# A graph layer's aggregation stage: who posts the updates of TensorE's mixer products

## The chip, the core and the metric

The kernel runs on one core of a Trainium2 chip. TensorE (PE in the profile) multiplies, with PEld for its weight loads; VectorE is DVE, ScalarE is ACT, GpSimd is POOL, SyncE is SP. Each engine has a sequencer of its own, which reads the instructions in order and hands matmuls, copies and so on to the engine; waits, register work and branches it does by itself. The metric is the device time of one execution in microseconds, lower is better.

## The reference

One layer of a graph network on 6250 nodes with 256 features, float32. Cut to what matters here:

```python
xn = layernorm(x)
# message passing: 100000 edges, sorted by dst
agg = segment_sum(xn[src], dst)
gnn = relu(xn @ W_self + (agg / max(deg, 1)) @ W_neigh + b)
# linear attention over all nodes, with a gate
k = softmax(k, axis=nodes); context = k^T v (per head); out = q @ context
gate = sigmoid(gelu(xn' @ Wg1 + bg1) @ Wg2 + bg2)
mix = out * gate @ Wproj + bproj
x = x + gnn + mix
# then a mixture of experts, routed by a graph attention over 131072 other edges
x = x + ffn(layernorm(x))
```

## The kernel before

The program is a row of stages; in one of them, `aggregate`, three strands run side by side, about from 105 to 1375 us of the execution.

**Message passing.** POOL gathers rows of the table `xn_tab` by indirect DMA (L857): one gather brings 128 rows (one "sub-step") into a ring of 4 x 8 slots, `msg`. ACT builds for each half of 8 sub-steps the one-hot matrices `hot` that say to which node of a tile each row belongs (`prep`, L1301 and L1303). TensorE multiplies the two (`steps`, L1125): two sub-steps are accumulated in one of four PSUM banks, and the last matmul of the pair counts up `s_mm`. DVE adds the bank to its tile of `acc` (`sums`, L879) and counts up `s_acc`, which frees the bank. One call `steps(.., u, u+4)` is four sub-steps, two banks. It has its addresses from a table: TensorE's sequencer loads them into registers (L1114, L1120), checks them, waits for the bank (L1123), and sets up each pair (L1125). POOL may overwrite a quarter of the ring once `s_mm` says that its rows were used (its wait is in the middle of each half, and in the same place it tells TensorE by `s_landed` that the half before has landed).

**The mixer** (the attention with its gate, and `x @ W_self`). Its products are put between the calls of `steps`, in program order, on two PSUM banks `mix[0]` and `mix[1]`:

- Stage B of this text, 220 to 565 us, 7 groups of 7 tiles: `kv(g, u)` (L1142 and L1145) makes k and v of 128 nodes in `mix[0]`. ACT reads them (`taken`, L1312 to L1314: the exponential, a copy, v scaled) and counts up `s_ev`; then `context` (L1152) multiplies the pair, and the next `kv` may write `mix[0]`. The order is `steps`, `kv(u)`, `context(u-1)`, `steps`, ..., with 8 calls of `steps` in a group.
- Stage C, 565 to 1190 us, 7 groups of 2 halves (4 and 3 tiles): `hidden` (L1162; DVE scales it, ACT makes the gelu), `gates` twice (L1170; ACT makes the sigmoid), `attention` twice (L1179; DVE multiplies it with the gate, `gated`, L887), then `output` for each tile (L1194 and L1196; DVE adds it up, `rowed`, L903). A call of `steps` stands ahead of each of them but for the second `attention`, 8 calls in a half.

After 1190 us the rest of the message passing runs alone (`rest`). The last matmul of each product carries the update of the semaphore that its reader waits for (`.then_inc`).

**A sort** of the other graph's edges on DVE, between its `sums`, with transposes on TensorE (`turn_from`, L304).

DVE and ACT do their work in one written order too: a `sums` that waits for `s_mm` holds up the `rowed` behind it.

Of the kernel before, what the change touches and what calls it, by code (L numbers as in the profile page):

```python
# [15 lines left out]
P = 128  # L16
# [669 lines left out]
def aggregate(c, a, t, acc, plan, xnT, r2, base):  # L686
# [8 lines left out]
    nc = c.nc  # L695
# [4 lines left out]
    with ctx:  # L700
# [16 lines left out]
        wg2 = sb("wg2", [GATE_H, D])  # L717
# [24 lines left out]
        for _, n in HALF:  # L742
# [10 lines left out]
        mix = [ps(f"mx_ps{i}", [P, 512]) for i in range(2)]  # L753
        s_w, s_wq, s_wqc, s_kv, s_ev, s_ctx, s_bd, s_m, s_msb = (c.sem("mx_" + n) for n in (
            "w", "wq", "wqc", "kv", "ev", "ctx", "bd", "m", "msb"))
# [5 lines left out]
        s_hgp, s_hg, s_gp, s_gate, s_at, s_prod, s_rows, s_copied = (c.sem("mx_" + n) for n in (  # L761
            "hgp", "hg", "gp", "gate", "at", "prod", "rows", "copied"))
# [20 lines left out]
        with nc.Block() as block:  # L783
# [324 lines left out]
            def _(pe):  # L1108
# [28 lines left out]
                def kv(g, u):  # L1137
                    at = (g * GT + u) * P
                    pe.wait_ge(s_ev, g * GT + u + 1)
                    b = mix[0]  # L1140
                    for k in range(KC):
                        nc.tensor.matmul(b[:, :], xnT[:, k, at:at + P], wqkv[:, k, D:3 * D], start=(k == 0), stop=False,  # L1142
                                         skip_group_check=True)

                    nc.tensor.matmul(b[:, 0:D], c.ones[0:1, :], ncm[:], start=False, stop=True,  # L1145
                                     skip_group_check=True).then_inc(s_kv, 1)

                def context(g, u):

# [6 lines left out]
                def hidden(g, i):  # L1156
                    n = HALF[i][1] * P
                    pe.wait_ge(s_in[i], 48 * g + 48)

                    pe.wait_ge(s_copied, g * GT + HALF[i][0] + GT)  # L1160
                    for k in range(KC):
                        last = nc.tensor.matmul(mix[0][0:GATE_H, 0:n], wg1[:, k, :], xT[i][:, k, :], start=(k == 0),  # L1162
                                                stop=(k == KC - 1))
                    last.then_inc(s_hgp, 1)

                def gates(g, i, h):
                    n = HALF[i][1] * P

                    pe.wait_ge(s_hg, 2 * g + i + 1)
                    nc.tensor.matmul(mix[1 - h][:, 0:n], wg2[:, h * P:(h + 1) * P], hg[:, 0:n], start=True,  # L1170
                                     stop=True).then_inc(s_gp, 1)

                def attention(g, i):
                    n = HALF[i][1] * P
                    for h in range(KC):

                        pe.wait_ge(s_gate, 4 * g + 2 * i + h + 1)
                        for k in range(KC):
                            last = nc.tensor.matmul(mix[1 - h][:, 0:n], m_sb[:, k, h * P:(h + 1) * P], xT[i][:, k, :],  # L1179
                                                    start=(k == 0), stop=(k == KC - 1))  # L1180
                        last.then_inc(s_at, 1)

                def output(g, i, j):
                    u = HALF[i][0] + j
                    at = j * P
                    b = mix[j % 2]
                    if j == 0:

                        pe.wait_ge(s_prod, 2 * g + i + 2)
                    elif j >= 2:  # L1190

                        pe.wait_ge(s_copied, g * GT + u - 1 + GT)
                    for k in range(KC):
                        nc.tensor.matmul(b[:, D:2 * D], xT[i][:, k, at:at + P], wself[:, k, :], start=(k == 0), stop=(k == KC - 1))  # L1194
                    for k in range(KC):
                        last = nc.tensor.matmul(b[:, 0:D], prod[:, k, at:at + P], wproj[:, k, :], start=(k == 0), stop=(k == KC - 1))  # L1196
                    last.then_inc(s_rows, 1)

                pe.sem_inc(s_mm, 2 * JB)
                pe.sem_inc(s_kv, GT)  # L1200
# [5 lines left out]
                                 skip_group_check=True)  # L1206
                pe.wait_ge(s_w, 16 * W_LOADS)
                for k in range(KC):
                    for h in range(KC):
                        last = nc.tensor.transpose(mix[0][:, h * D + k * P:h * D + (k + 1) * P], wqkv[:, k, h * P:(h + 1) * P], c.ident[:])  # L1210
                last.then_inc(s_wq, 1)
                nc.tensor.transpose(psS[0:TILES, 0:P], r2[:], c.ident[:])
                for k in range(KC):
                    last = nc.tensor.matmul(psS[0:GATE_H, 512:513], wg1[:, k, :], ln_b[:, k:k + 1], start=(k == 0), stop=(k == KC - 1))
# [13 lines left out]
                for p in range(LANE_PAIRS):  # L1228
                    for k in range(QUART):
                        for i in range(2):  # L1230
# [4 lines left out]
                            elif at == CHUNKS:  # L1235
                                pe.wait_ge(s_kmax, KC * CHUNKS + 1)
                                for h in range(KC):
                                    last = nc.tensor.transpose(psS[0:1, h * P:(h + 1) * P], cmax[:, h:h + 1], c.ident[:])
                                last.then_inc(s_k, 1)
                pe.wait_ge(s_kmax, KC * CHUNKS + 2)  # L1240
                for g in range(GROUPS):
                    for u in range(GT + 1):
                        steps(LANE_PAIRS + g, u // 2, u % 2 * 4, u % 2 * 4 + 4)
                        if u < GT:
                            kv(g, u)
                        if u:
                            context(g, u - 1)

                pe.wait_ge(s_bd, 1)
                for k in range(KC):  # L1250
                    for h in range(KC):
                        last = nc.tensor.matmul(mix[0][:, k * D + h * P:k * D + (h + 1) * P], wqT[:, h, k * P:(k + 1) * P], ctxbd[:, h, :],
                                                start=True, stop=True)
# [4 lines left out]
                for g in range(GROUPS):  # L1258
                    for i in range(2):
                        p = C_PAIR + 2 * g + i  # L1260
                        steps(p, 0, 0, 4)
                        if i == 0:
                            srt.turn_from(pe, 0, 2 * g + 1)
                        hidden(g, i)
                        steps(p, 0, 4, 8)
                        gates(g, i, 0)
                        steps(p, 1, 0, 4)
                        gates(g, i, 1)
                        steps(p, 1, 4, 8)
                        attention(g, i)  # L1270
                        for j in range(4):
                            steps(p, 2 + j // 2, j % 2 * 4, j % 2 * 4 + 4)
                            if j < HALF[i][1]:
                                output(g, i, j)
                            if i == 0 and j == 2:
                                srt.turn_from(pe, 1, 2 * g + 2)
# [1232 lines left out]
```

## Time and profile before

| | |
|---|---|
| three runs | 2709.36, 2723.76, 2723.77 us, median 2723.76 |
| the profiled execution | 2707.9 us, its span 2706.1 us |
| busy, of the span | PE 72%, PEld 50%, DVE 44%, ACT 34%, POOL 55% |
| mean granted TensorE clock | 0.827 |
| matmuls | 7528 records; a float32 product is recorded as two |

The page of the profile gives one execution. The busy share of an engine is the part of the span in which one of its instructions was in work. For an instruction that waited, the profile names what ended the idle time of its engine ("releaser"); "issue" means that no wait ended just then, the sequencer was only now ready with it; "remote" means that the semaphore was counted up at that time, but that no instruction that counts it up had ended near then. The ends of matmuls are modelled.

### The profile page before, as it was taken

The numbers are of one execution on the slowest core, as the hardware profiler recorded it, in microseconds if no ns is written. First come the engines' busy times: TensorE is split into PE (matmuls) and PEld (weight loads), VectorE is DVE, ScalarE is ACT, GpSimd is POOL, SyncE is SP. The second block draws the span as 40 slices with busy tenths as digits, with TensorE's granted clock in tenths as the row PEclk, the third lists the DMA queues.
The fourth block names the chain that finished last, engine by engine and source line by source line (L and its number), as shares of the span: only waits on it lengthen the run. The fifth ranks groups of instructions, "written<-read, shape, count | busy, mean of one in ns | idle before, by whom it ended". The sixth has DMA issues, their size and how long they took to land. (4 is left out here: it accounts for less than half of the span.)

```text
span 2706.1 us, 26735 instructions
## 1 busy us (share of the span) xinstructions
PE 1941.8 (72%) x7528; PEld 1341.2 (50%) x7528; DVE 1194.9 (44%) x2204; ACT 907.0 (34%) x1994; POOL 1480.2 (55%) x1512
## 2 busy tenths in 40 slices
PE   5687878876677777765455888788888788784235
PEld 4454545454455554543345555456555555553223
DVE  6353222345455555543386223324235143346368
ACT  3432444444444444443323222222323222222124
POOL 2455655666566666676602566666666666561510
PEclk9888988998888898887665899999998889897555
DMA  5443222244343434353358221212222112215544
GB/s 182 142 134 114 87 70 79 84 118 137 113 137 111 139 120 143 105 166 123 93 161 277 82 49 36 70 36 49 57 50 56 38 48 56 51 36 172 160 149 152
DMA packets 197046, 282.83 MB, mean 105 GB/s; under 512 B 43024, under 2 KB 147443, under 8 KB 195762
## 3 DMA queue, kind: packets, MB, share of 16 engines
q0 software_dynamic: 61280, 115.13, 16.6%
q1 hardware_dynamic: 97218, 121.11, 13.5%
q10 hardware_dynamic: 38416, 44.96, 5.1%
q8 instruction: 67, 1.10, 0.2%
q14 instruction: 65, 0.53, 0.1%
HBM read 195.29 MB, written 85.80 MB: 104 GB/s over the span
## 5 line engine op out<-in xcount | busy, mean ns | idle before, releaser
L857 POOL DMA_INDIRECT ag_msg<-xn_tab,step_src x784 | 784.8, 1001 | 462.1 <-issue 218.3
L1814 POOL DMA_INDIRECT edge_rows<-hx_d,gat_src x648 | 623.7, 962 | 357.1 <-issue 180.6
L1125 PE MATMUL ag_ps<-ag_msg,ag_hot 128*128 x1760 | 491.5, 428 | 117.4 <-issue 61.0
L2002 PE MATMUL ex_psY<-co_rows 128*128 128x256 f32 x1568 | 416.0, 426 | 130.9 <-ACT co_rows L2056 70.2
L1125 PEld LDWEIGHTS ag_ps<-ag_msg,ag_hot 128*128 128x128 f32 x1760 | 364.4, 215 | 244.2 <-issue 187.6
L879 DVE TENSOR_TENSOR acc<-acc,ag_ps 128x257 f32 x440 | 186.0, 423 | 638.3 <-remote 276.5
L2002 PEld LDWEIGHTS ex_psY<-co_rows 128*128 128x128 f32 x1568 | 332.2, 215 | 212.3 <-ACT co_rows L2056 79.9
L1990 PE MATMUL ex_psF<-co_rows 128*128 128x448 f32 x896 | 353.9, 551 | 46.2 <-DMA ex_b<-in_b_dram 24.9
L1301 ACT ACTIVATE gat_self<-iota_row,step_nloc 128x128 f32<-128x128 f32 x880 | 270.4, 388 | 304.4 <-issue 164.7
L1928 DVE TENSOR_TENSOR hi_one_low<-hi_numbers,hi_low 128x2048 bf16<-128x2048 f32 x64 | 146.4, 2287 | 498.9 <-remote 416.1
L1990 PEld LDWEIGHTS ex_psF<-co_rows 128*128 128x128 f32 x896 | 171.2, 194 | 212.5 <-issue 165.3
L2056 ACT COPY co_rows<-ex_psY 128x256 f32<-128x256 f32 x196 | 71.3, 373 | 471.7 <-PE ex_psY L2002 245.7
L2049 ACT ACTIVATE co_rows<-ex_psF,ex_b 128x448 f32<-128x448 f32 x224 | 137.8, 633 | 252.8 <-PE ex_psF L1990 167.8
L1142 PE MATMUL mx_ps<-wqkv,xnT 128*128 128x512 f32 x196 | 103.3, 653 | 47.2 <-ACT gat_dst L1314 37.6
L1303 ACT ACTIVATE ag_hot<-gat_self,ones 128x1024 f32<-128x1024 f32 x110 | 126.3, 1149 | 13.0 <-issue 5.3
L1929 DVE TENSOR_TENSOR hi_one_high<-hi_numbers,hi_high 128x1568 bf16<-128x1568 f32 x64 | 114.0, 1781 | 0.0
L1194 PE MATMUL mx_ps<-wself,xnT 128*128 128x256 f32 x196 | 57.8, 421 | 39.2 <-DVE xnT L903 27.6
L218 DVE TENSOR_TENSOR gatsort_keys<-gatsort_keys 128x512 f32<-128x512 f32 x117 | 80.3, 687 | 1.0
L1142 PEld LDWEIGHTS mx_ps<-wqkv,xnT 128*128 128x128 f32 x196 | 40.1, 210 | 80.9 <-ACT gat_dst L1314 40.8
L219 DVE TENSOR_TENSOR gatsort_keys<-gatsort_keys 128x512 f32<-128x512 f32 x117 | 80.1, 684 | 0.0
L1312 ACT ACTIVATE gat_dst<-mx_ps 128x256 f32<-128x256 f32 x49 | 18.8, 383 | 179.0 <-remote 88.4
L1224 PE MATMUL srt_ps<-xnT,wqkv 128*128 128x448 f32 x112 | 49.7, 588 | 20.9 <-DVE bmax L916 15.0
(377 smaller groups left out, 2000.0 us busy)
## 6 DMA issues: line engine op xcount, KB each, us to landing
y_d<-co_rows ACTq DMA_DIRECT2D x28, 896.0 KB
co_rows<-y_d SPq DMA_DIRECT2D x28, 896.0 KB, 9.5
ag_msg<-xn_tab,step_src POOLq DMA_INDIRECT x784
xnT<-base_d SPq DMA_DIRECT2D x7, 1792.0 KB
edge_rows<-hx_d,gat_src POOLq DMA_INDIRECT x648
base_d<-xnT ACTq DMA_DIRECT2D x7, 1024.0 KB
sums_d<-edge_rows SPq DMA_DIRECT2D x5, 1344.0 KB
xg<-in_x_dram SPq DMA_DIRECT2D x7, 896.0 KB, 5.7
```

The lines of the kernel that those rows point to most:

```text
L857: pool.indirect_dma_start(msg[:, q, u, 0:D], None, c.xn_tab, bass.IndirectOffsetOnAxis(ap=t.idx[:, at:at + 1], axis=0)).then_inc(s_g[q], 16)
L879: V.tensor_tensor(own, own, bank[(at // JOIN + u) % BANKS][:, 0:ROWW], ALU.add).then_inc(s_acc, 1)
L1125: last = nc.tensor.matmul(bank[(at + r) % BANKS][:, 0:ROWW], hot[:, k, u0 + r * JOIN + j, :], ring[:, j * ROWW:SLOTS * ROWW][:, ds(places[ ...
L1142: nc.tensor.matmul(b[:, :], xnT[:, k, at:at + P], wqkv[:, k, D:3 * D], start=(k == 0), stop=False, skip_group_check=True)
L1301: A.activation(dif[:, u, :], c.iota_row[:], ACT.Abs, bias=t.nloc[:, ds(half * SHALF + u, 1)])
L1303: A.activation(hot[:, k], dif[:], ACT.Relu, bias=c.ones[:, 0:1], scale=-1.0).then_inc(s_hot, 1)
L1814: pool.indirect_dma_start(G[:, j % RING, w, :], None, c.hx_d, bass.IndirectOffsetOnAxis(ap=plan.idx[:, at + w:at + w + 1], axis=0)).then_i ...
L1928: V.tensor_tensor(one_low[:, k % 2], bcast(numbers, 1, HIST), bcast(low[:, at], 2, P), ALU.is_equal)
L1929: V.tensor_tensor(one_high[:, k % 2], bcast(numbers[:, 0:HIGHS], 1, HIST), bcast(high[:, at], 2, HIGHS), ALU.is_equal).then_inc(s_one, 1)
L1990: last = nc.tensor.matmul(psF[i % FB][:, 0:HB], w1[:, e, k, (i // 2) * P:(i // 2 + 1) * P], yT[:, k, (i % 2) * HB:(i % 2 + 1) * HB], start ...
L2002: last = nc.tensor.matmul(bank[:, 0:D], hh[:, k].rearrange("p a b -> p (a b)")[:, u * P:(u + 1) * P], w2[:, e, k, :], start=(k == 0), stop ...
L2049: nc.scalar.activation(hh[:, i // 2, i % 2, :], psF[i % FB][:, 0:HB], ACT.Gelu, bias=b1[:, e * HC + i // 2:e * HC + i // 2 + 1]).then_inc( ...
```

## The change

In five products the last matmul no longer carries the update. Instead TensorE's sequencer waits until the engine has drained, and then counts the semaphore up itself.

```diff
@@ kv
                     nc.tensor.matmul(b[:, 0:D], c.ones[0:1, :], ncm[:], start=False, stop=True,
-                                     skip_group_check=True).then_inc(s_kv, 1)
+                                     skip_group_check=True)
+                    pe.drain()
+                    pe.sem_inc(s_kv, 1)
@@ hidden
-                    last.then_inc(s_hgp, 1)
+                    pe.drain()
+                    pe.sem_inc(s_hgp, 1)
@@ gates
-                    nc.tensor.matmul(mix[1 - h][:, 0:n], wg2[:, h * P:(h + 1) * P], hg[:, 0:n], start=True,
-                                     stop=True).then_inc(s_gp, 1)
+                    nc.tensor.matmul(mix[1 - h][:, 0:n], wg2[:, h * P:(h + 1) * P], hg[:, 0:n], start=True, stop=True)
+                    pe.drain()
+                    pe.sem_inc(s_gp, 1)
@@ attention
-                        last.then_inc(s_at, 1)
+                        pe.drain()
+                        pe.sem_inc(s_at, 1)
@@ output
-                    last.then_inc(s_rows, 1)
+                    pe.drain()
+                    pe.sem_inc(s_rows, 1)
```

The updates of `steps` (`s_mm`), of `context` (`s_ctx`) and of the sort's transposes stay on their matmuls. No instruction changes its place.

## Rows read from the trace of the kernel before

**Rows 1.** The gathers by their line: ns min/median/max, first and last start in us.
```profile
L857 POOL DMA_INDIRECT ag_msg<-xn_tab,step_src x784: 940/946/2321, 105.6 to 1351.0; - x196
```

**Rows 2.** Windows: length, busy us of PE, PEld, DVE, ACT, POOL, granted clock, DMA, GB/s.
```profile
220.00:565.00 345.00, 277.75 (x962) 170.25 (x960) 104.94 (x213) 153.41 (x410) 207.25 (x209) 0.89 0.31 90
565.00:1190.00 625.00, 464.02 (x1625) 319.40 (x1624) 327.26 (x582) 267.72 (x570) 399.20 (x394) 0.85 0.41 123
```

**Rows 3.** Timeline of TensorE, one unit of stage B: start, us, instruction, idle before.
```profile
403.71 1.88 PE L1142 MATMUL mx_ps<-wqkv,xnT 128*128 128x512 f32 x4
405.52 0.69 PE L1145 MATMUL mx_ps<-ncm,ones 1*128 1x256 f32 x2
406.14 0.71 PE L1152 MATMUL mx_ps<-gat_dst 128*128 128x129 f32 x4
406.69 1.90 PE L1125 MATMUL ag_ps<-ag_msg,ag_hot 128*128 x8
408.43 1.88 PE L1142 MATMUL mx_ps<-wqkv,xnT 128*128 128x512 f32 x4
```

**Rows 4.** Timeline of TensorE, a stall of stage B.
```profile
379.82 0.69 PE L1145 MATMUL mx_ps<-ncm,ones 1*128 1x256 f32 x2
...
380.99 1.90 PE L1125 MATMUL ag_ps<-ag_msg,ag_hot 128*128 x8
394.42 1.22 PE L1142 MATMUL mx_ps<-wqkv,xnT 128*128 128x512 f32 x1 [11.52 <-ACT gat_dst L1314]
```

**Rows 5.** Timeline of ACT in the same stretch.
```profile
393.52 0.38 ACT L1312 ACTIVATE gat_dst<-mx_ps 128x256 f32<-128x256 f32 x1 [12.92 <-remote]
```

**Rows 6.** Timeline of POOL in the same stretch.
```profile
389.85 0.95 POOL L857 DMA_INDIRECT ag_msg<-xn_tab,step_src  x1 [0.30 <-issue]
404.68 1.17 POOL L857 DMA_INDIRECT ag_msg<-xn_tab,step_src  x1 [13.89 <-PE ag_ps L1125]
```

**Rows 7.** Who waited for whom in stage B: us in total, times, longest.
```profile
ACT gat_dst L1312 <- remote: 88.4, 13, 17.6
DVE acc L879 <- remote: 86.1, 17, 12.6
POOL ag_msg L857 <- PE ag_ps L1125: 63.2, 13, 13.9
```

**Rows 8.** Who waited for whom in stage C.
```profile
POOL ag_msg L857 <- PE ag_ps L1125: 78.6, 25, 10.8
PE mx_ps L1170 <- ACT xnT L1320: 29.1, 5, 8.6
PE mx_ps L1194 <- DVE xnT L903: 27.6, 8, 11.6
PE mx_ps L1162 <- DVE xnT L903: 15.7, 4, 8.7
```

**Rows 9.** TensorE's sequencer at the lines of steps: ns min/median/max of each instruction.
```profile
L1114 PEldq TENSOR_LOAD <-step_table x203: 502/713/3027, 120.7 to 1366.0; - x102
L1120 PEldq TENSOR_LOAD <-step_table x203: 472/477/1504, 121.3 to 1366.6; - x102
L1120 PEldq FUSED_REGOPS  x203: 151/151/162, 121.9 to 1367.1; - x102
L1123 PEldq EVENT_SEMAPHORE  x203: 51/51/51, 122.2 to 1367.4; - x102
L1125 PEldq FUSED_REGOPS  x228: 42/44/46, 222.3 to 553.0; - x114
```

**Rows 10.** Timeline of TensorE in stage C, a product that had to be waited for.
```profile
758.95 1.12 PE L1170 MATMUL mx_ps<-xnT,wg 64*128 64x512 f32 x2 [1.07 <-issue]
760.75 1.56 PE L1125 MATMUL ag_ps<-ag_msg,ag_hot 128*128 x6 [0.68 <-issue]
```

**Rows 11.** TensorE's drain at the aggregation's end, by its line.
```profile
L783 PEldq DRAIN  x1: 1268/1268/1268, 1372.4 to 1372.4; - x1
```

**Rows 12.** Timeline of TensorE, its last matmuls before that drain's end.
```profile
1371.60 2.00 PE L1125 MATMUL ag_ps<-ag_msg,ag_hot 128*128 x8 [1.94 <-DVE acc L879]
```

## The prediction

> **What bounds the kernel now.** I read the page first, then windows over the aggregation, the timelines of single units, and the waits. Only the aggregation is touched, and no other stage runs beside it, so the change is worth what it makes stages B and C longer or shorter; a shift of their end moves everything after it alike.
>
> POOL issues 784 gathers of 0.95 us [rows 1] with 0.30 between them [rows 6], so 1.25 us each or 980 us in all, from 105.6 to 1351.0 us [rows 1], a stretch of 1245 us. It is not the bound alone: in stages B and C it waited 63.2 and 78.6 us for matmuls of `steps` [rows 7, 8]. TensorE is busy 278 of 345 us in stage B and 464 of 625 us in stage C [rows 2]; its idle time there is 67 + 161 = 228 us. A unit of stage B without a stall takes 408.43 - 403.71 = 4.72 us, back to back [rows 3], against 5.0 us of POOL for the four gathers that it uses. 49 such units would be 231 us, so a good part of stage B's 345 us is stalls.
>
> The stalls look odd. In one, the last matmul of `kv` ends at 380.51 us [rows 4], but ACT, which has nothing else to wait for, starts its read at 393.52, 13.0 us later, and the profile calls the releaser "remote" [rows 5]: the semaphore counted up then, with no matmul near. TensorE in turn sits 11.5 us for ACT [rows 4]. POOL made gathers back to back up to 390.8 [rows 6]. The updates that ride on matmuls thus arrive late at times, while TensorE itself goes on (the eight matmuls of `steps` started at 380.99). Waits that end so cost ACT 88.4 us and DVE 86.1 us in stage B [rows 7]. This is what the change can win.
>
> The Trainium skill (PSUM — Partial Sum Buffer, "Engine vs sequencer instructions") says that updates attached to an engine's instruction fire when it completes, and wants them there; the trace disagrees in this stage by 13.0 us. By that rule the change would win nothing and pay all of the price below.
>
> **The change, part by part.** It removes 49 + 14 + 28 + 28 + 49 = 168 updates from matmuls (kv, hidden, gates, attention, output) and adds as many drains and sequencer updates.
>
> *The update itself.* A sequencer's semaphore instruction takes 0.05 us (the 51 ns of L1123) [rows 9]. A drain shown ends at 1372.4 + 1.27 = 1373.67, and the matmuls before it at 1373.60 [rows 11, 12]: it adds under 0.1 us after the last matmul. An update of the mixer then reaches ACT or DVE some 0.1 us after the product, if the drain does not wait for late updates too and the sequencer's own are on time. Neither is to be seen before; the rivals take that up.
>
> *The lost run-ahead.* This is the price. The sequencer's work for one call of `steps` is, up to its first matmul, 713 + 477 + 151 + 51 + 44 = 1436 ns of instructions [rows 9], and with the gaps between them 1.80 us, read where a product had to wait until 758.95 and its sequencer with it: the next `steps` began at 760.75, 0.68 us after the product's end although nothing was to be waited for [rows 10]. In a flowing unit these 1.8 us are hidden, since the sequencer does them while earlier matmuls run [rows 3]. A drain holds the sequencer at the end of the product, so that all of it is bare, about 1.9 us with drain and update. Whatever product stands between is hidden behind it: after `kv` comes `context`, whose own start after the drain and 0.7 us of matmuls [rows 3] leave some 1.6 us of added length.
>
> - kv, stage B: 49 x 1.6 = 78 us.
> - hidden 14, gates 28, the second attention 14, output 49: 105 followed by `steps`, x 1.9 = 200 us.
> - the first attention, 14, followed by matmuls without table loads: what is left of 1.9 us without the 1.44 us of sequencer work, 0.46, so 6 us.
>
> Sum 284 us more of TensorE's time. Where the product had to be waited for anyway, part of this is paid already (the 0.68 us of rows 10), and it counts as idle time now.
>
> *What takes it up.* If all idle time of the two stages were filled, they would last 278 + 78 = 356 instead of 345 us and 464 + 206 = 670 instead of 625 us: +11 and +45, together +56 us. Stalls are idle time that ends with POOL's pause, not with TensorE's work, so bare sequencer time ahead of one costs little, and the mixer's own late updates go. But not all idle time can be filled: the updates of `steps` stay on their matmuls, and DVE and ACT meet those waits in their written order, ahead of the `rowed` and `gated` that TensorE waits for (27.6 and 15.7 us on L903, 29.1 us on ACT) [rows 8]. I leave 14 us of it, which makes +70 us.
>
> *The bounds.* Above: nothing is taken up, +284 us. Below: the granted clock is 0.89 and 0.85 in the two stages [rows 2], a mix of its full and its half level; had it been full, the busy time would be about 278 x 0.89 = 247 and 464 x 0.85 = 394 us, and with the drains 325 and 600 us against 345 and 625: -45 us. Long idle stretches were followed by the slow level (the `steps` after the stall), short ones of 1.9 us need not be.
>
> DVE, ACT and POOL get no new work. POOL finds the slots freed later where TensorE is later, and pauses more; behind a pause the updates are on time (the two matmul updates of rows 3 released ACT at once), which works against the stalls and is part of why I let most idle time be filled. The rest of the aggregation after 1190 us has no mixer and only shifts.
>
> **The numbers.** The sum goes against the profiled execution: 2708 + 70 = 2778 us. The runs lie at 2709 and twice at 2724, so half their spread above it: **2785 us**. What a measurement can tell from no change is about 0.5%, 14 us.
>
> **Rivals.**
>
> 1. *Faster.* The mixer's updates come at once, the chain product, reader, next product no longer breaks, TensorE is never idle for long and keeps its full clock. The stages then run at the lower bound, -45 us: 2663 in the profile, about 2670. For it: 88.4 us of waits of ACT on late updates in stage B alone [rows 7]. Against it: even without a single stall the drained unit of stage B is 4.7 + 1.6 = 6.3 us, and a group of 8 calls about 47 us against 49 now, so that little is there to win, and the late `s_mm` remain. It decides where the clock returns to full level in both stages. Chance 0.20.
> 2. *No change.* The filled idle time and half of the clock's return meet: +56 - 50 = about 0, 2720. Chance 0.13.
> 3. *The change does not do what it says.* The drain waits until the late updates of `steps` are out as well, or TensorE's sequencer posts into the same jam. Then each late update stops the whole of TensorE at the next drain, where it now ran on for a unit (the eight matmuls of rows 4). The skill's page says a drain waits until the engine is fully idle, and leaves open whether unposted updates count. Half of the idle time at most is then filled: 284 - 114 = +170 us, 2886; with a quarter, 284 - 57 = +227, 2943. For it: in the drain shown the last update was not late, so nothing speaks against. Chance 0.19.
>
> My own case, slower by 15 to 130 us with 2785 in the middle, gets 0.48. The first rival gives faster 0.20, the second same 0.13, mine and the third slower 0.67. The range leaves out the lower half of the first rival and the far end of the third: 2685 to 2930 us.
>
> **What would show it.** In the timeline of TensorE a unit of stage B from `kv` to `kv` of 6.2 to 6.5 us instead of 4.72, with an idle time of 1.0 to 1.3 us before L1125 put down to "issue", and after each output 1.8 to 2.0 us of it; "PE ag_ps L1125 <- issue" as the longest wait of both stages, near 200 us. ACT L1312 <- remote gone. DVE acc L879 <- remote still there. Both stages within a few us of 360 and 670. Wrong would be: a drain after whose matmuls the update still comes microseconds late (then rival 3), an idle time before L1125 under 1 us after outputs (the price is too high), or a granted clock of 0.95 and more with stages under 340 and 615 us (rival 1).

## The result, and the profile after

The changed kernel takes 2915.99 us (median of 4 runs, 2904.72 to 2933.57) against 2723.77: ratio 1.0746, 95% interval 1.07 to 1.0793. Slower, as forecast, but by 192 us where 61 were forecast. The profiled execution has a span of 2915.2 us. Ratios, here and below, are those on record, taken over fast runs alone; the quotient of two medians can differ from them by up to 0.4% (here it is 1.0706).

The windows of stages B and C, with the boundaries put at the last product of each (length, busy us of PE, PEld, DVE, ACT and POOL, granted clock, DMA share, GB/s), first before the change, then after it:

```profile
220.00:572.00 352.00, 282.14 (x978) 173.70 (x976) 107.33 (x218) 153.41 (x410) 211.53 (x213) 0.89 0.31 92
572.00:1185.00 613.00, 457.45 (x1601) 314.40 (x1600) 324.45 (x577) 267.72 (x570) 391.14 (x385) 0.86 0.41 122
```
```profile
220.00:617.00 397.00, 304.66 (x980) 189.12 (x979) 108.01 (x218) 153.75 (x410) 211.13 (x213) 0.88 0.28 82
617.00:1409.00 792.00, 542.01 (x1600) 355.35 (x1598) 327.68 (x582) 267.05 (x570) 395.94 (x390) 0.80 0.32 96
```

Stage B is 45 us longer, stage C 179. Two things stand out: the idle time of TensorE, and its busy time, which should not have changed at all, since the matmuls are the same; in stage C its clock is 0.80 instead of 0.86.

A unit of stage B in TensorE's timeline (start, us, instruction, idle before it), to be held against [rows 3]:

```profile
302.58 0.69 PE L1145 MATMUL mx_ps<-ncm,ones 1*128 1x256 f32 x2
303.36 0.71 PE L1154 MATMUL mx_ps<-gat_dst 128*128 128x129 f32 x4
305.30 2.00 PE L1125 MATMUL ag_ps<-ag_msg,ag_hot 128*128 x8 [1.23 <-issue]
307.13 1.88 PE L1142 MATMUL mx_ps<-wqkv,xnT 128*128 128x512 f32 x4
308.94 0.69 PE L1145 MATMUL mx_ps<-ncm,ones 1*128 1x256 f32 x2
```

From `kv` to `kv` it is 308.94 - 302.58 = 6.36 us, where 6.2 to 6.5 were forecast. Behind an output, three units in stage C (eight matmuls of `steps` take 3.41 us in the first, most of it at the slow level of the clock, and 2.00 us in the second):

```profile
932.55 3.41 PE L1125 MATMUL ag_ps<-ag_msg,ag_hot 128*128 x8 [1.92 <-issue]
...
939.89 2.00 PE L1125 MATMUL ag_ps<-ag_msg,ag_hot 128*128 x8 [1.93 <-issue]
...
945.54 5.42 PE L1125 MATMUL ag_ps<-ag_msg,ag_hot 128*128 x16 [1.92 <-issue]
```

1.92 us, where 1.8 to 2.0 were forecast. All such idle time of TensorE from 220 to 606 us, from 606 to 1410 us (us in total, times, longest), and, for later, in both stages of e5 below, the changed kernel once more:

```profile
PE ag_ps L1125 <- issue: 77.4, 51, 10.4
```
```profile
PE ag_ps L1125 <- issue: 249.9, 107, 13.9
```
```profile
PE ag_ps L1125 <- issue: 267.1, 154, 3.9
```

That is 327 us, where the forecast had near 200 and the longest wait of both stages; DVE's wait for the matmuls of `steps` is longer in stage B. Who waited for whom there:

```profile
ACT gat_dst L1318 <- PEq L1147: 207.1, 44, 17.9
DVE acc L879 <- PE ag_ps L1125: 205.2, 83, 6.0
POOL ag_msg L857 <- PE ag_ps L1125: 120.4, 22, 9.7
...
DVE acc L879 <- remote: 23.7, 6, 11.4
```

ACT's waits on "remote" [rows 7] are gone, and L1147, the drain, is what releases it; but the longest such wait is still 17.9 us, and POOL waits twice as long as before. Why, the drain of `hidden` tells, first by its line and then with TensorE and DVE around it:

```profile
L1166 PEldq DRAIN  x14: 1468/3835/14842, 613.1 to 1363.3; - x14
```
```profile
1057.84 1.93 PE L1164 MATMUL mx_ps<-xnT,wg 128*64 128x512 f32 x4
1073.63 1.65 PE L1125 MATMUL ag_ps<-ag_msg,ag_hot 128*128 x3 [13.86 <-issue]
```
```profile
1071.85 0.68 DVE L910 TENSOR_TENSOR xnT<-mx_ps,xnT 64x512 f32<-64x512 f32 x1 [12.69 <-PEq L1166]
```

The product ends at 1059.77, the update of the sequencer behind it releases DVE at 1071.85, 12.1 us later. The drain, too, can be late. By the trace 21 of the 168 drains end over 0.1 us after the last matmul ahead of them and 12 over 1 us; all lateness together is 65 us.

### The profile page after: what moved, and what is told of

The parts are those of the page before. It is cut to its first block and busy times, and to the rows that moved or that the text cites. A ratio compares the mean times of both kernels' runs of the same rounds, so it can differ in the third digit from the quotient of the medians.

```text
span 2915.2 us, 26903 instructions
## 1 busy us (share of the span) xinstructions
PE 2038.8 (70%) x7528; PEld 1390.0 (48%) x7528; DVE 1197.2 (41%) x2204; ACT 905.3 (31%) x1994; POOL 1479.6 (51%) x1512
## 3 DMA queue, kind: packets, MB, share of 16 engines
q1 hardware_dynamic: 97218, 121.11, 12.6%
## 5 line engine op out<-in xcount | busy, mean ns | idle before, releaser
L857 POOL DMA_INDIRECT ag_msg<-xn_tab,step_src x784 | 784.1, 1000 | 676.2 <-PE ag_ps L1125 425.5
L1125 PE MATMUL ag_ps<-ag_msg,ag_hot 128*128 x1760 | 581.4, 489 | 409.5 <-issue 363.9
L1125 PEld LDWEIGHTS ag_ps<-ag_msg,ag_hot 128*128 128x128 f32 x1760 | 403.8, 239 | 577.6 <-issue 508.2
L879 DVE TENSOR_TENSOR acc<-acc,ag_ps 128x257 f32 x440 | 186.2, 423 | 817.5 <-PE ag_ps L1125 543.9
L1876 DVE TENSOR_TENSOR edge_rows<-edge_rows,gs_ex 128x1792 f32<-128x1792 f32 (+2 forms) x7 | 11.9, 1702 | 118.8 <-ACT gs_ex L2071 118.8
```

The costliest lines, as they stand in the source:

```text
L857: pool.indirect_dma_start(msg[:, q, u, 0:D], None, c.xn_tab, bass.IndirectOffsetOnAxis(ap=t.idx[:, at:at + 1], axis=0)).then_inc(s_g[q], 16)
L879: V.tensor_tensor(own, own, bank[(at // JOIN + u) % BANKS][:, 0:ROWW], ALU.add).then_inc(s_acc, 1)
L1125: last = nc.tensor.matmul(bank[(at + r) % BANKS][:, 0:ROWW], hot[:, k, u0 + r * JOIN + j, :], ring[:, j * ROWW:SLOTS * ROWW][:, ds(places[ ...
```

## The experiments

All ratios are to runs of the kernel before beside them. One thing surprised at once: in the first two sets the kernel before takes 2263 and 2266 us, in the last two 2687 and 2717, though the median instruction takes as long (a gather 0.946 us, the addition on L879 0.423 us, a matmul record of `steps` 0.380 us in either). The four sets ran on four chips, each on one, so that chip, host and hour cannot be told apart; the chip of the first pair is not on record. I call them places without and with late updates, because that is what tells them apart, as e5 and e9 show.

### First set: before at 2263 us

**e1_drain_only**, in all five products alike:

```diff
-                    last.then_inc(s_rows, 1)
+                    last.then_inc(s_rows, 1)
+                    pe.drain()
```

> The five products keep their update on the last matmul, and TensorE's sequencer only drains behind it; nothing else is changed. Theory (the drain's lost run-ahead is the price, the sequencer's own update a return): the price is paid whole and the late updates are back, so slower than the changed kernel, 2940 to 3000 us, with about 1.9 us of idle time before the steps behind each output. Rival (the sequencer's update is itself the slow part): like the kernel before, or at most 2800 us.

Measured: 2574.46 us, ratio 1.1381 (1.1352 to 1.1409). The absolute range was set for the other place; as a ratio it was 1.08 to 1.10, and the result lies above that too. Nor is it slower than the change: e5 below gives the change there 1.1377: with the update on the matmul or by the sequencer, the same. Where no update is late the drain alone is the price, and the sequencer's update is worth nothing.

**e2_kv_only**: `drain` and `sem_inc` behind `kv`, the other four as before.

> Only kv drains and posts by the sequencer; the 119 products of stage C keep their update on the matmul. The profile of the changed kernel has stage B 41 us longer and stage C 180 us longer. Theory (the two stages pay for themselves): 2750 to 2765 us, 25 to 45 us above before. Rival (the drains in stage B let POOL and TensorE enter stage C in another phase, and part of the 180 us comes from there): 2790 us or more.

Measured: 2355.72 us, ratio 1.043 (1.0405 to 1.0455). Outside both absolute ranges; e5 and e6 show that the stages do pay for themselves. Each pays more in this place: stage B is 377 us here against the 278 us of e6, 99 more, where the first pair had 45.

**e3_ahead_drained** splits `steps` into the register loads and the rest, and asks for the next call's registers before the product:

```diff
-                def steps(p, k, u0, u1):
+                def ready(p, k, u0, u1):
...
+                    count = pe.value_load(t.half[:, ds(at + n - 1, 1)], min_val=1, max_val=HALVES)
+                    return half, at, n, k, u0, places, count
...
-                        steps(p, 0, 4, 8)
+                        call = step(call)
                         gates(g, i, 0)
```

`step(call)` runs a call and returns the registers of the next.

> As the changed kernel, but the register loads and checks of the next call of steps are issued before the product and its drain instead of behind them. Theory (the bare 1.4 us of table loads per drain is the price): the idle time before steps behind an output falls from 1.92 to about 0.5 us, stages B and C lose some 49 x 1.2 + 105 x 1.4 = 206 us, less where POOL becomes the bound: 2690 to 2740 us. Rival (the drain itself or a jam of updates is the price): 2850 us or more.

**e4_ahead_only**: the same without the drains.

> The kernel before with the same early register loads and no drain. Theory: the loads are hidden in flowing units already, so within 15 us of before, a little faster where a product had to be waited for (0.68 us of idle time each): 2695 to 2725 us. Rival (late updates dominate what happens after each wait): no difference at all.

Measured: e3 2265.66 us, ratio 1.0012 (1.0001 to 1.0023); e4 2259.19 us, 0.9987 (0.9974 to 1.0). As ratios, both are as the theory had it. The 168 drains are still there in e3; without the bare register loads behind them the 14% are gone. Stages B and C of e3:

```profile
188.00:467.00 279.00, 263.65 (x980) 157.97 (x979) 108.84 (x218) 153.78 (x410) 212.73 (x217) 0.99 0.40 117
467.00:992.00 525.00, 449.12 (x1601) 286.05 (x1600) 327.30 (x581) 267.16 (x570) 398.87 (x385) 0.95 0.48 143
```

### Second set: before at 2266 us

**e5_change_again**: the changed kernel.

> The changed kernel itself once more, beside the kernel before, since the first experiments ran where the kernel before takes 2263 us and no update of a matmul is late. Theory A (late updates belong to the chip or host, and the change pays its lost run-ahead everywhere): where before is near 2263 us, the change has nothing to win and costs the whole 284 us less little, ratio 1.11 to 1.14; where before is near 2720 us again, 1.07. Rival B (late updates were chance in one profile, the slow-down does not depend on them): ratio 1.07 in either case.

Measured: 2580.39 us, ratio 1.1377 (1.1346 to 1.1409), theory A; no wait of stages B and C ends "remote". Its two stages, then stage B undrained (e6) and stage C undrained (e2):

```profile
189.00:572.00 383.00, 308.01 (x982) 192.90 (x982) 109.00 (x218) 155.02 (x413) 216.78 (x219) 0.88 0.30 87
572.00:1313.00 741.00, 538.12 (x1599) 353.60 (x1598) 326.42 (x580) 267.77 (x570) 395.96 (x389) 0.81 0.34 102
```
```profile
188.00:466.00 278.00, 262.49 (x982) 166.12 (x981) 108.74 (x218) 154.10 (x413) 213.99 (x211) 0.97 0.39 115
```
```profile
563.00:1072.00 509.00, 427.45 (x1601) 305.50 (x1600) 325.33 (x579) 267.20 (x570) 385.46 (x377) 0.91 0.49 146
```

The whole price without late updates can be read here: 383 - 278 = 105 and 741 - 509 = 232, together 337 us (the part behind stage C gives some back, so that the run is 314 longer). Of it 45.5 + 110.7 = 156 us are busy time of the same matmuls, at 0.88 and 0.81 of the clock instead of 0.97 and 0.91; the other 181 are idle time. All 168 drains of this run end within 0.03 us of the last matmul.

**e6_c_only**: the change without its first part (`kv`).

> Only the 119 products of stage C drain and post by the sequencer; kv keeps its update on the matmul. Theory A: the two stages add up; with kv alone at a ratio of 1.043 the rest is stage C, so the change's ratio less 0.043, 1.07 to 1.10 where no update is late; there 206 us by count. Rival (the stages share a bound, so that one of them alone brings the whole): as the change.

Measured: 2472.8 us, ratio 1.091 (1.0873 to 1.0948). With e2, 0.091 + 0.043 = 0.134 against 0.138: the stages add up.

**e7_pool_pauses**, on the kernel before:

```diff
+                        if h and u == 0:
+                            pool.wait_ge(s_g[(h - 1) % QUART], 16 * SHALF * ((h - 1) // QUART + 1))
```

> The kernel before, but POOL also waits at the start of each half of eight gathers until the half before has landed, so that at most four to eight gathers run without a pause. Theory A (an update of a matmul is late when POOL has made more than four gathers without a pause): where updates are late they become rarer, under 10% of them over 0.3 us instead of 30%; the pauses cost POOL up to 98 x 2.5 = 245 us and give back part of the stalls: ratio 0.97 to 1.04. Where no update is late, POOL is the bound and the pauses cost in full: ratio 1.06 to 1.11. Rival (late updates have nothing to do with POOL): the share of late updates stays.

Measured: 2462.68 us, ratio 1.0861 (1.0831 to 1.0891): here the pauses cost in full.

**e8_all_by_sequencer**: e3, and the two updates of a call of `steps` move behind the product's drain:

```diff
-                        last.then_inc(s_mm, 1)
+                        if post:
+                            last.then_inc(s_mm, 1)
...
                         hidden(g, i)
+                        pe.sem_inc(s_mm, 2)
```

> The early register loads, the changed kernel's drains, and the two updates of each call of steps that has a drained product behind it are posted by the sequencer with that product's. Theory A: no update of stages B and C rides on a matmul but for context and the sort. Where updates are late this is the kernel without stalls: ratio 0.90 to 0.97. Where none is late it is the early-loads kernel with drains, 1.00, or a little more since banks come free later: 1.00 to 1.03. Rival (the sequencer's updates are as late as the matmuls'): ratio above 1.0 where updates are late.

Measured: 2324.24 us, ratio 1.0253 (1.0219 to 1.0287), inside the range for this place.

### Third set: before at 2687 us, with late updates

**e9_before_again**: the kernel before.

> The kernel before itself, for a profile of it from where the experiments run. Theory A: where it takes about 2265 us, stage B and C last about 278 and 509 us as in the two half-changes, POOL's gathers run without pauses over 1 us but for a few, and no update of a matmul releases its reader late; ratio 1.00. Rival B: the late updates are there too, rarer.

Measured: 2668.95 us, ratio 0.9966 (0.9922 to 1.001). The late updates are back with the long time. Its waits in stages B and C:

```profile
DVE acc L879 <- remote: 168.3, 34, 12.5
...
POOL ag_msg L857 <- PE ag_ps L1125: 116.7, 33, 10.3
...
ACT gat_dst L1312 <- remote: 76.8, 10, 17.9
```

**e10_kv_filled**, on e2:

```diff
                         if u:
                             context(g, u - 1)
+                        if u < GT:
+                            for _ in range(3):
+                                nc.tensor.matmul(psS[:, 512:768], c.ident[:], wqkv[:, 0, 0:256], start=True, stop=True)
```

> As the kernel with the drain behind kv alone, and behind context three matmuls of 128x256 on spare columns are added in each of 49 units, 1.3 us of work that fills the 1.2 us in which TensorE waits for its sequencer; their result is read by nobody. Theory C (the idle gaps lower TensorE's granted clock, and that is the part of the price which the count of gaps leaves out, some 25 of 100 us in stage B): the clock of stage B returns from 0.90 to 0.97 or more, its busy time per record falls, and although work is added stage B is 15 to 45 us shorter than the 377 us of kv alone: ratio 1.02 to 1.035 against 1.043. Rival D (the clock is set by something else): stage B is as long or up to 60 us longer, ratio 1.043 to 1.07.

Measured: 2700.9 us, ratio 1.012 (1.0035 to 1.0206). Stage B of it, and of e16, which is the same without the filling:

```profile
215.00:607.00 392.00, 341.27 (x1275) 224.88 (x1273) 108.57 (x218) 154.55 (x412) 211.15 (x214) 0.95 0.28 83
```
```profile
225.00:624.00 399.00, 305.87 (x981) 190.26 (x980) 108.27 (x218) 154.03 (x411) 212.25 (x214) 0.88 0.28 81
```

The clock rose from 0.88 to 0.95 as theory C said. With 294 more matmul records, which took 79.1 us themselves, the busy time is only 35 us larger: the 472 records of `steps` took 124.1 us instead of 151.0. Stage B is 7 us shorter, under the 15 to 45 forecast, and two profiles of the kernel before differ by more (352 and 341 us); the whole is no faster than e16. So the gaps do lower the clock, but filling them is no gain here.

**e11_rows_on_matmul**: the change without its part on `output`.

> The change without its fifth part: output keeps its update on the matmul and does not drain; the other 119 drains stay. Theory A (each drain with steps behind it costs 1.9 us, and more by the clock): 49 x 1.9 = 93 us less than the change, up to 140 with the clock: where before is 2265 us, 2440 to 2490, ratio 1.076 to 1.10. Rival (the drains of the gate chain bring the loss of stage C, those of the outputs stand where TensorE would wait anyway): ratio above 1.12.

Measured: 2819.3 us, ratio 1.0526 (1.044 to 1.0612). The ranges were for the other place; against the change's 1.0746, 49 of 168 drains less save 0.022, some 60 us, two thirds of the 93 by count. Its stage C is 724 us against 792.

**e12_all_by_sequencer_again**: e8.

> The kernel with early register loads in which the sequencer posts the updates of steps too, once more. It was meant for a place with late updates. Where before takes about 2720 us: ratio 0.90 to 0.97, since hardly an update is left to be late in stages B and C. Where before takes 2265 us: 1.025 as measured, stage B 291 and stage C 571 us.

Measured: 2783.62 us, ratio 1.0376 (1.0298 to 1.0453). The theory failed: with hardly a matmul left whose update can be late, the kernel is slower than before. In its trace the first product of an `attention` and the drain's line:

```profile
1112.85 1.97 PE L1191 MATMUL mx_ps<-xnT,gat_src 128*128 128x512 f32 x4
1124.26 3.78 PE L1191 MATMUL mx_ps<-xnT,gat_src 128*128 128x512 f32 x4 [9.44 <-issue]
```
```profile
L1193 PEldq DRAIN  x28: 1533/1975/11335, 611.4 to 1278.6; - x28
```

The product ends at 1114.82; the next starts at 1124.26, and between them stands nothing but the drain and a wait for `s_gate`. The drains before it ended with everything done, and since then no matmul that carries an update was issued. So what is late is not the update but TensorE's completion, and a drain waits for it like a reader does. By the trace 49 of the 168 drains end over 0.1 us after the last matmul ahead of them, 166 us in all. POOL meanwhile gathers back to back:

```profile
1112.49 1.38 POOL L857 DMA_INDIRECT ag_msg<-xn_tab,step_src  x1 [0.30 <-issue]
...
1121.68 0.95 POOL L857 DMA_INDIRECT ag_msg<-xn_tab,step_src  x1 [0.30 <-issue]
```

### Fourth set: before at 2717 us, with late updates

**e13_ahead_drained_again** is e3, **e14_ahead_only_again** is e4.

> The change with early register loads, once more, for a place where updates of matmuls are late (before near 2700 us). Theory A (the bare table loads are most of the price, and the mixer's own late updates are won back): stages B and C lose at least 200 of the change's 404 + 792 us: ratio 0.97 to 1.02 there. Rival (the drains wait for late completions, so that they cost as much as they win): 1.02 to 1.05, as the kernel in which the sequencer posts everything. Where before takes 2265 us: 1.00 as measured.

> The kernel before with early register loads, once more for a place with late updates. After each stall TensorE restarts without 0.7 to 1.3 us of bare register loads: some 60 restarts, ratio 0.975 to 1.0. Rival: no difference, 0.995 to 1.005. Where before takes 2265 us: 1.00 as measured.

Measured: e13 2800.35 us, ratio 1.0276 (1.0197 to 1.0355); e14 2709.52 us, 0.9967 (0.993 to 1.0005). The rival of e13 holds. e3's drains cost 12 us where no completion is late (stages B and C of 279 + 525 us against e4's 275 + 517), and 135 us here:

```profile
217.00:595.00 378.00, 292.52 (x982) 180.18 (x980) 108.52 (x218) 154.29 (x412) 211.29 (x214) 0.87 0.30 86
595.00:1301.00 706.00, 493.57 (x1601) 314.74 (x1600) 326.51 (x582) 269.62 (x570) 388.70 (x389) 0.84 0.36 107
```
```profile
220.00:570.00 350.00, 284.29 (x981) 171.95 (x980) 108.19 (x218) 153.40 (x411) 208.83 (x214) 0.88 0.32 93
570.00:1169.00 599.00, 451.62 (x1599) 314.24 (x1598) 323.55 (x577) 267.23 (x570) 389.87 (x385) 0.86 0.42 125
```

(first e13, then e14: 378 + 706 against 350 + 599). A drain does not go round a late completion; it stops TensorE for it. By the trace 52 of e13's 168 drains are over 0.1 us late, 218 us in all, and none of e3's in these stages.

**e15_pool_pauses_again** is e7.

> The kernel before with a second wait of POOL in each half of eight gathers, so that at most eight run without a pause, once more for a place with late updates. Theory A (a completion of TensorE is late when POOL has made four gathers or more without a pause): long lateness, over 5 us, goes, stages B and C lose stalls and gain pauses: ratio 0.96 to 1.03 there, and fewer than a tenth of the updates late instead of a quarter. Rival (POOL has nothing to do with it): the share stays and the ratio is 1.06 to 1.09. Where before takes 2265 us: 1.086 as measured.

Measured: 2685.07 us, ratio 0.9848 (0.9789 to 0.9907), the only kernel with an interval below 1 in a place with late updates; it loses 8.6% in the other. Waits in its stages B and C (its lines are two further down):

```profile
DVE acc L881 <- remote: 65.4, 23, 5.8
...
ACT gat_dst L1314 <- remote: 12.6, 4, 4.1
```

Against e9 the longest falls from 12.5 to 5.8 and from 17.9 to 4.1 us, the sums from 168.3 to 65.4 and from 76.8 to 12.6. Part of that is only a change of name, since DVE's waits put down to "issue" rose from 73.6 to 133.8 us. The length of the stages is surer. Here, and in e7:

```profile
202.00:525.00 323.00, 277.91 (x980) 174.10 (x980) 107.94 (x218) 152.40 (x408) 206.39 (x210) 0.92 0.34 99
525.00:1154.00 629.00, 461.99 (x1600) 321.94 (x1601) 326.42 (x581) 267.12 (x570) 396.31 (x389) 0.87 0.40 120
```
```profile
200.00:523.00 323.00, 277.74 (x981) 176.15 (x980) 108.56 (x218) 152.75 (x408) 207.60 (x210) 0.91 0.34 99
523.00:1154.00 631.00, 458.72 (x1599) 322.59 (x1598) 327.49 (x582) 267.89 (x570) 397.69 (x390) 0.86 0.40 120
```

952 and 954 us: with the pauses the place makes no difference to these stages, while the kernel before needs 178 us more in the one than in the other. So the pauses take away what lateness costs, and cost as much themselves: e9 has 954 us too and e14, in this same place, 949. Where the 1.5% comes from, the profiles don't show. That fewer than a tenth of the updates would be late is not borne out either: of DVE's waits that end with a matmul or "remote", 23 of 179 are "remote", against 34 of 165 in e9.

**e16_kv_only_again** is e2.

> Drain and the sequencer's update behind kv alone, once more. Where updates are late: the kernel with the same drain and filled gaps had a stage B of 392 us at a clock of 0.95 and a ratio of 1.012; without the filling stage B should be 395 us, as in the change and in the kernel without drained outputs, at 0.88 to 0.90, busy less by the added matmuls: ratio 1.01 to 1.025. Rival (the filling was of use): 1.03 or more. Where before takes 2265 us: 1.043 as measured.

Measured: 2758.38 us, ratio 1.0128 (1.006 to 1.0196), with the stage B shown at e10.

## Why the prediction was right and wrong

**The direction and the mechanism held.** The lost run-ahead is the main price: the unit of 6.36 us, the 1.92 us behind outputs, and e3 against e5, where the same drains without bare register loads take the ratio from 1.138 to 1.001.

**The step that failed is "what takes it up", in its busy time.** It counted the busy time as fixed at 278 + 464 us and let 214 of 284 us disappear in idle time. In the first pair of profiles the busy time of unchanged matmuls rose by 22 + 85 = 107 us instead of 0, and the idle time of the two stages went from (352 - 282) + (613 - 457) = 226 to (397 - 305) + (792 - 542) = 342 us, +117 before rounding, instead of +70. Together 224, the 45 + 179 us. So 107 of the 154 us between forecast and result in these stages are busy time.

Most of that is the clock. Weighed by TensorE's busy time, the clock in the traces is 0.90 and 0.87 before, 0.87 and 0.75 after; by an estimate from these, some 87 of the 107 us go to the slow level. I had the clock only on the side of gain, with "short ones of 1.9 us need not be" followed by the slow level. The other 20 us remain at any clock: TensorE's work now falls into 226 busy stretches where it had 100. e3 shows this part alone, with a higher clock than e4 (0.99 and 0.95 against 0.98 and 0.92) and still 713 us of busy time against 685. Where no update is late, 156 of 337 us are busy time.

The overlap itself was well judged: of 226 us idle before and 327 us bare now, 342 remain, so that 211 were taken up where 214 were forecast.

**"The update itself" failed too.** Under 0.1 us after the product is right for all drains of e5, and for 147 of 168 in the changed kernel; the others are late, up to 12.0 us, and add 65 us. That is the mechanism of the third rival. Without that lateness 262 us are bare, against 267 in e5 and the 284 of the forecast. Nor had ACT "nothing else to wait for" in the stall of [rows 4]: it also waits for the update of an earlier `context`, which the change left on its matmul. The price of that rival was thought of as idle time not filled; e13 against e3 shows it by itself, 135 - 12 = 123 us. The rival's guess that the sequencer's own update may jam is not borne out: behind the late drain shown, the reader started 0.1 us after the drain's end.

**What the change won.** The stages B and C cost 787 us undrained without lateness and 965 with it (352 + 613), 178 us more; drained as in the change 1124 and 1189, 65 more, which is what the late drains add up to. It would be wrong to call the 113 us won back: e13, with the same drains and a fast TensorE, loses 280 us to lateness (1084 against 804). The likely reason why the change suffers less is that TensorE is so slow that POOL pauses for it, 425.5 us in all in place of 166.1:

```profile
L857 POOL DMA_INDIRECT ag_msg<-xn_tab,step_src x784: 940/946/2502, 108.0 to 1566.9; - x196
its engine sat idle before it (us, times) until:
  PE ag_ps L1125: 425.5, 70
```

Pauses take away what lateness costs (e15). That they do so in the changed kernel is argued from e15, not tried.

**The range** ended at 2930 for a median of 2916 and held it; the forecast inside it was a third of the loss. My own case ended at 130 us, and the time lay where the third rival had it (2886 to 2943). That the range held it owes much to luck: it was drawn down there for late drains, which cost 65 us, and not for the busy time, which cost 107.

**Open.** Why completions of TensorE are late in some places and not in others, and what in POOL's gathers delays them, no run here tells. The ends of matmuls are modelled, so it is open as well whether a product is really finished late or only seen late. And the traces of the late places are short of records: that of the kernel before holds 13183 updates of semaphores and no landing time for the gathers, that of e4 31320 and a landing time. The issues of the gathers in the two:

```profile
ag_msg<-xn_tab,step_src POOLq DMA_INDIRECT x784
```
```profile
ag_msg<-xn_tab,step_src POOLq DMA_INDIRECT x784, 2.8
```

So "remote" and "issue" in the late places are in part names of waits whose record is missing; start times, drains and lengths of stages do not hang on that. Every run on record comes with a clock, so it was traced, and whether the tracing has a part in the lateness stands untested.

## What to carry to other kernels

A drain costs what the sequencer would have done meanwhile: count its register loads and waits behind the drain, and move them ahead of it, before asking whether the drain is worth it. Where completions are late it waits for them too (65 us here, 218 us in e13). Where a change puts gaps of 1 to 2 us into every unit, look at the busy time and the clock of the matmuls around them too; here they cost 107 us, nearly as much as the 117 us of added idle time. When an update arrives late, find out whether the message or the completion is late, since only the first can be sent another way.

## What the hardware showed

Unexpected: the kernel before takes 2263 to 2266 us in two places and 2687 to 2724 us in others, with equal median durations of its instructions. In the late places completions of TensorE come up to 13 us late while POOL issues gathers without a pause. Up to the first gather of the aggregation the places do not differ (105 us, and 101 in e9, against 102 in e4). Stages B and C hold 178 us of the difference, less than half. Behind the aggregation, where POOL makes 648 gathers of another kind, the kernel before and e4, which are alike there, take:

```profile
1374.00:2706.00 1332.00, 960.38 (x4086) 678.65 (x4086) 592.53 (x933) 350.86 (x680) 672.90 (x701) 0.81 0.32 90
```
```profile
1146.00:2260.00 1114.00, 877.36 (x4088) 634.85 (x4086) 593.25 (x934) 355.07 (x680) 680.72 (x701) 0.84 0.38 108
```

That is 218 us more, which no change of this text touches. Cutting the gathers of the aggregation by a pause in every half is worth 1.5% in the one place (0.9 to 2.1%) and costs 8.6% in the other.
